# Two adjacency products and a sparse attention correction on one core: staging all columns at once, and product two's chunks placed whole

## What is computed

```python
# layer 0: scores exist only at the pairs; the diagonal is 1e-7, absent edges are -inf
attn = softmax(where(adj == 0, -inf, scores), axis=2)      # 8 heads
x = layernorm(x + (attn.sum(0) / 8) @ x)
# layer 1, on the result
S = (adj + adj.T) * 0.5 + eye;  deg = S.sum(1);  An = deg[:, None]**-0.5 * S * deg[None, :]**-0.5
x = layernorm(x + (adj @ An) @ x)
```

## Time and profile before

| what | us |
|---|---|
| median of 3 runs | 257.16 (256.54 to 257.19) |
| span of the profiled execution | 256.0 |
| PE busy / weight loads | 196.7 / 87.7 |
| DVE busy | 149.1 |
| ACT busy | 73.1 |
| POOL busy | 93.5 |
| bytes read and written in HBM | 25.66 and 8.86 MB, 135 GB/s over the span |

### The profile page before, as it was taken

One profiled execution on the slowest core, in us unless ns is written; L12 is line 12 of the kernel. 1 busy time (PEld: TensorE's weight loads), 2 busy tenths in 40 slices (PEclk: granted clock), 3 DMA queues, 4 the chain that ended last, 5 costly groups with the idle time before them and its releaser, 6 DMA issues.

```text
span 256.0 us, 2880 instructions
## 1 busy us (share of the span) xinstructions
PE 196.7 (77%) x874; PEld 87.7 (34%) x874; DVE 149.1 (58%) x351; ACT 73.1 (29%) x119; POOL 93.5 (37%) x107
## 2 busy tenths in 40 slices
PE   0003999999585376966999999879669999999950
PEld 0001344444132122422564434334224444444420
DVE  7826646429799369945610008769484445387871
ACT  2005384044762698330003130311032222001010
POOL 3677877777778777730011005601010000000000
PEclk9999999999799687995958999999999999999996
DMA  4971886189751399930002001911139100022230
GB/s 148 382 226 25 321 283 172 44 323 289 281 198 52 90 340 300 328 123 28 0 3 82 0 0 30 300 54 41 41 102 305 72 0 3 0 104 102 82 123 24
DMA packets 16623, 34.69 MB, mean 135 GB/s; under 512 B 5148, under 2 KB 5274, under 8 KB 16610
## 3 DMA queue, kind: packets, MB, share of 16 engines
q1 hardware_dynamic: 13074, 30.74, 35.7%
q0 software_dynamic: 3536, 3.79, 5.2%
HBM read 25.66 MB, written 8.86 MB: 135 GB/s over the span
## 4 chain that ended last, share of the span: by engine, by line
POOL 31%; PE 27%; DVE 19%; issue 13%; DMA 5%; ACT 2%; DVEq 1%; POOLq 0%
POOL kept L421 31%; PE ps L598 16%; DVE stats L1129 3%; PE ps L684 3%; DVE xs L1126 3%; DMA kept<-in_adj_t,at_idx 2%; DVE xs L1133 2%; PE ps L664 2%; PE ps L609 2%; PE ps L719 2%; ACT std L587 1%; DMA work<-v_rows 1%; DMA v_rows<-work 1%; DVE mv L1130 1%; PE ps L681 1%
## 5 line engine op out<-in xcount | busy, mean ns | idle before, releaser
L421 POOL DMA_INDIRECT kept<-in_adj_t,at_idx x79 | 79.8, 1010 | 28.5 <-issue 23.8
L598 PE MATMUL ps<-terms,at 128*128 128x512 f16 x264 | 61.4, 392 | 3.2 <-ACT at L494 2.3
L609 PE MATMUL ps<-terms,at 128*128 128x512 f16 x220 | 52.0, 399 | 10.4 <-ACT u L499 10.4
L598 PEld LDWEIGHTS ps<-terms,at 128*128 128x128 f16 x264 | 26.4, 101 | 36.5 <-issue 3.7
L609 PEld LDWEIGHTS ps<-terms,at 128*128 x220 | 22.2, 102 | 39.9 <-issue 16.9
L598 PE MATMUL ps<-terms,bm 128*128 128x512 f16 x110 | 30.4, 446 | 4.3 <-DVE terms L836 4.3
L609 PE MATMUL ps<-terms,bm 128*128 128x512 f16 x132 | 29.3, 379 | 0.0
L598 PEld LDWEIGHTS ps<-terms,bm 128*128 128x128 f16 x110 | 12.1, 112 | 21.7 <-issue 12.9
L609 PEld LDWEIGHTS ps<-terms,bm 128*128 128x128 f16 x132 | 12.8, 98 | 16.4 <-issue 1.7
L553 ACT ACTIVATE u<-ps 128x512 f32<-128x512 f32 x11 | 6.0, 601 | 37.7 <-PE ps L598 25.1
L848 DVE TENSOR_TENSOR bm<-bm,at 128x1408 f16<-128x1408 f16 x11 | 9.8, 890 | 11.6 <-ACT bm L506 11.4
(11 more groups left out here) (222 smaller groups left out, 207.9 us busy)
## 6 DMA issues: line engine op xcount, KB each, us to landing
stage<-in_adj_t SPq DMA_DIRECT2D x10, 677.0 KB, 6.8
stage<-in_adj SPq DMA_DIRECT2D x10, 677.0 KB, 5.0
u_rows<-u SPq DMA_DIRECT2D x10, 257.5 KB
x_rows<-xs SPq DMA_DIRECT2D x10, 256.0 KB
xs<-x_rows SPq DMA_DIRECT2D x10, 256.0 KB
out<-xs SPq DMA_DIRECT2D x10, 256.0 KB
xs<-in_x SPq DMA_DIRECT2D x2, 768.0 KB, 4.7
kept<-in_adj_t,at_idx POOLq DMA_INDIRECT x79
```

Source lines behind the costliest of these rows:

```text
L421: pool.indirect_dma_start(out=kept[:, c:c + 1], out_offset=None, in_=adj_flat, in_offset=bass.IndirectOffsetOnAxis(ap=at_idx[:, c:c + 1], ...
L598: m = pe.matmul(ps[:, i, :], matrix[:, k, i * P:(i + 1) * P], terms[:, s, k, :], start=first and s == 0, stop=last and s == 1)
L609: m = pe.matmul(ps[:, bass.ds(bank_of(i), 1), :].rearrange("p o d -> p (o d)"), matrix[:, k, bass.ts(i, P)], terms[:, s, k, :], start=(k = ...
```

## The change

It has six parts. (1) Each of the 11 column loads has a place of its own (three `stage` slots, four in `u`, five in `bm`), so all are issued right behind x without a wait; the rows use `stage` and `work`. (2) The element-wise load of the diagonal goes; DVE takes it from `at` with a masked product and a reduce per group (`own_entries`). The 11 additions of 2 on the diagonal become three (`add_identity`). (3) DVE makes the gather index before anything else that isn't needed, in 4 instructions in place of 10, and moves the rest of that work, some memsets and `slot_cols` behind the last low term of product one. (4) The scale goes to all partitions by one f32 matmul of ones with a diagonal. (5) Product two's terms are written into `u`, each chunk over its own f32 row, and its results into `xs`; ACT's `high_terms(m)` waits for the stores of that part of `u`. (6) PE does all eleven `bx_step`s and three whole chunks before the ranks, one chunk before the packing, one before q and k, none in loops 2 and 3, and one at the start of loop 4.

```diff
-X_LOADS = [(0, 3), (3, 7), (7, C)]
+X_LOADS = [(0, 4), (4, 8), (8, C)]
-STEPS_TO_RANKS, STEPS_TO_PACK = 6, 9
-BEFORE_QK, AFTER_QK, IN_LOOP2, IN_LOOP3, IN_LOOP4 = 1, 1, 1, 1, 1
-ROWS_V = (1, 3, 5)
+BEFORE_RANKS, BEFORE_PACK, BEFORE_QK, IN_LOOP4 = 3, 1, 1, 1
+ROWS_V = (3, 7)
+STAGE_T = [("u", 0), ("u", 1), ("u", 2), ("u", 3), ("bm", 0), ("bm", 1), ("bm", 2), ("bm", 3), ("bm", 4), ("stage", 0), ("stage", 1)]
+STAGE_R = [("stage", 2), ("work", 0), ("work", 1), ("work", 2), ("stage", 0), ("stage", 1), ("stage", 2), ("work", 0), ("work", 1), ("work", 2), ("stage", 0)]
...
+        def z_term(i, s):
+            return u[:, i, 0:H].bitcast(f16)[:, s * H:(s + 1) * H]
...
 # SP
             for k in range(C):
-                if k >= STAGES:
-                    j = k - STAGES
-                    sp.wait_ge(at_odd if j % 2 else at_even, j // 2 + 1)
                 rows = P if k < C - 1 else TAIL
-                sp.dma_start(stg[0:rows, k % STAGES, 0:N], adj_t[k * P:k * P + rows, :]).then_inc(stage_in[k % STAGES], 16)
-            sp.dma_start(a_ii[:, 0:C - 1]..., bass.AP(tensor=adj_t.tensor, ...)).then_inc(aii_in, 16)
-            sp.dma_start(a_ii[0:TAIL, C - 1:C], ...).then_inc(aii_in, 16)
+                sp.dma_start(staged(STAGE_T[k])[0:rows, :], adj_t[k * P:k * P + rows, :]).then_inc(col_in[k], 16)
+            for r in range(C):
+                before = [q for q in range(r) if STAGE_R[q] == STAGE_R[r]]
+                if before:
+                    rows_cast(sp, before[-1])
+                elif STAGE_R[r] in STAGE_T:
+                    k = STAGE_T.index(STAGE_R[r])
+                    sp.wait_ge(at_odd if k % 2 else at_even, k // 2 + 1)
+                rows = P if r < C - 1 else TAIL
+                sp.dma_start(staged(STAGE_R[r])[0:rows, :], adj[r * P:r * P + rows, :]).then_inc(row_in[r], 16)
...
 # ACT
-            act.wait_ge(scale_ready, 1)
             for k in range(C):
-                act.activation(terms[:, 0, k, :], xs[:, k, :], ACT.Copy, scale=scale[:, 0:1]).then_inc(x_hi, 1)
                 if k % 2 == 0:
                     (cast of column k)
+                if k == 0:
+                    act.wait_ge(scale_ready, 1)
+                else:
+                    act.activation(terms[:, 0, k, :], xs[:, k, :], ACT.Copy, scale=scale[:, 0:1]).then_inc(x_hi, 1)
...
-            for r in (0, 2, 4):
+            for r in ROWS_S[:6]:
                 adj_rows(r)
             for i in GROUP_A:
                 ax_evacuate(i, i)
+            for r in ROWS_S[6:]:
+                adj_rows(r)
...
             def high_terms(m):
+                u_kept(act, m)          # waits for the stores of u of this part
                 act.wait_ge(x1_ready, PARTS[m][1])
                 for i in range(*PARTS[m]):
-                    act.activation(terms[:, 0, i, :], xs[:, i, :], ACT.Copy, scale=dinv_x[:, i:i + 1]).then_inc(xt_hi, 1)
-            adj_rows(6)
-            adj_rows(7)
-            adj_rows(8)
+                    act.activation(z_term(i, 0), xs[:, i, :], ACT.Copy, scale=dinv_x[:, i:i + 1]).then_inc(xt_hi, 1)
             ax_evacuate(6, ax_bank(6))
-            adj_rows(9)
-            adj_rows(10)
-            ax_evacuate(7, ax_bank(7))
             roots_of(0)
             dense_norm(0)
+            ax_evacuate(7, ax_bank(7))
+            high_terms(0)
             ax_evacuate(8, ax_bank(8))
-            ax_evacuate(9, ax_bank(9))
-            ax_evacuate(10, ax_bank(10))
-            high_terms(0)
             roots_of(1)
             dense_norm(1)
             high_terms(1)
+            ax_evacuate(9, ax_bank(9))
+            ax_evacuate(10, ax_bank(10))
             roots_of(2)
...
 # PE
-            for k in range(0, STEPS_TO_RANKS):
-                pe.wait_ge(bm_ready, k + 1)
+            for k in range(C):
+                if k in (0, 6):
+                    pe.wait_ge(bm_ready, 1 if k == 0 else 3)
                 bx_step(k)
+            bx_chunks(0, BEFORE_RANKS)
             pe.wait_ge(base_in, 1)
             (ranks)
-            pe.wait_ge(bm_ready, C)
-            for k in range(STEPS_TO_RANKS, STEPS_TO_PACK):
-                bx_step(k)
+            bx_chunks(BEFORE_RANKS, BEFORE_PACK)
             (packing)
-            for k in range(STEPS_TO_PACK, C):
-                bx_step(k)
             pe.wait_ge(l1_slots, tiles)
-            bx_chunks(0, BEFORE_QK)
+            bx_chunks(BEFORE_RANKS + BEFORE_PACK, BEFORE_QK)
...
 # DVE, behind the memsets of raw, xs, ones, at and col_a
+            dve.wait_ge(pairs_in, 32)
+            main(dve.tensor_scalar(pg[:, :, :], raw[:, :, :], 0.0, float(N), ALU.is_lt, ALU.mult))
+            main(dve.tensor_tensor(pf[:, :, :], raw[:, :, :], pg[:, :, :], ALU.add))
+            main(dve.scalar_tensor_tensor(ok2[:, :], pf[:, :, 1], float(N), pf[:, :, 0], ALU.mult, ALU.add))
+            dve.tensor_scalar(at_idx[:, :], ok2[:, :], 0.0, float(N * N - 1), ALU.max, ALU.min).then_inc(idx_ready, 1)
...
+            (behind the low terms of product one: memsets of bm, row_a, ones16, onecol, rank16;
+             two16 = 2 * ident16; ok, ok2, code; slot_cols)
...
+            def add_identity(lo, hi):
+                dve.wait_ge(v_step, main.n)
+                dve.tensor_tensor(blocks(bm, lo, hi), blocks(bm, lo, hi), each(two16, hi - lo), ALU.add).then_inc(bm_ready, 1)
+            def own_entries(lo, hi):
+                own = ...
+                main(dve.tensor_tensor(own, blocks(at, lo, hi), each(ident16, hi - lo), ALU.mult))
+                main(dve.tensor_reduce(a_ii[:, lo:hi], own, AX.X, ALU.add))
...
-            two_way(0, 6)
+            for lo, hi in ((0, 6), (6, C - 1), (C - 1, C)):
+                own_entries(lo, hi)
+            two_way(0, 7)
+            add_identity(0, 6)
             dense_rows(0)
-            two_way(6, C)
+            two_way(7, C)
+            add_identity(6, C - 1)
+            add_identity(C - 1, C)
             dense_finish(0)
```

More of the change, by code:

```diff
@@ L116, in build, with staged, columns_in, rows_in @@
         row_x0 = words[:, 18 * P + 4 * H:18 * P + 5 * H]
-        stg = stage[:, :].rearrange("p (s n) -> p s n", s=STAGES)
+        homes = {
+            "stage": stage[:, :],
+            "work": work[:, :].bitcast(f32),
+            "u": u[:, :, :].rearrange("p c d -> p (c d)"),
+            "bm": bm[:, :, :].rearrange("p c n -> p (c n)").bitcast(f32),
+        }
+        def staged(place):
+            home, slot = place
+            return homes[home][:, slot * NP:slot * NP + N] if home == "stage" else homes[home][:, slot * N:(slot + 1) * N]
+        def columns_in(eng, k):
+            eng.wait_ge(col_in[k], 16)
+        def rows_in(eng, r):
+            eng.wait_ge(row_in[r], 16)
         w_sb = stage[:, 0:2 * HC * H].rearrange("p (w c n) -> p w c n", w=2, c=HC)
@@ L380, in _ @@
                     rows = P if i < C - 1 else TAIL
-                    sp.dma_start(u_rows[i * P:i * P + rows, :], u[0:rows, i, :]).then_inc(u_stored, 16)
+                    sp.dma_start(u_rows[i * P:i * P + rows, :], u[0:rows, i, :]).then_inc(u_stored[m], 16)
                 for i in range(lo, hi):
@@ L453, in _ @@
             pool.wait_ge(x1_stored, 16 * C)
-            pool.wait_ge(u_stored, 16 * C)
+            for m in range(len(PARTS)):
+                u_kept(pool, m)
             take_indices(0, tiles + 1, row_i)
@@ L552, in bx_evacuate @@
                 act.wait_ge(bx_done, i + 1)
-                act.activation(u[:, i, 0:H], ps[:, i % 5, :], ACT.Copy).then_inc(bx_out, 1)
-            act.wait_ge(u_stored, 16 * C)
-            bx_evacuate(0)
+                act.activation(xs[:, i, :], ps[:, i % 5, :], ACT.Copy).then_inc(bx_out, 1)
+            act.wait_ge(x1_stored, 16 * C)
+            act.wait_ge(xt_lo, C)
+            early = len(AHEAD) + BEFORE_RANKS + BEFORE_PACK
+            for i in range(early):
+                bx_evacuate(i)
             act.activation(warm[:, :], eps_c[:, :], ACT.Exp).then_inc(warmed, 1)
@@ L566, in _ @@
                 act.activation(k_sb, ps[:, 6, :], ACT.Copy).then_inc(l1_k_sb, 1)
-            for i in AHEAD[1:]:
+            for i in range(early, C - IN_LOOP4):
                 bx_evacuate(i)
@@ L579, in _ @@
                 with act.If(t < 1):
-                    for i in BESIDE[-IN_LOOP4:]:
+                    for i in range(C - IN_LOOP4, C):
                         bx_evacuate(i)
@@ L590, in _, with together_step @@
         def _(pe):
-            def together_step(k, first, last, bank_free, ready, matrix, done, chunks=GROUP_A):
+            def together_step(k, first, last, bank_free, ready, matrix, term, done, chunks=GROUP_A):
                 ready(k)
@@ L597, in together_step @@
                     for s in range(2):
-                        m = pe.matmul(ps[:, i, :], matrix[:, k, i * P:(i + 1) * P], terms[:, s, k, :],
+                        m = pe.matmul(ps[:, i, :], matrix[:, k, i * P:(i + 1) * P], term(k, s),
                                       start=first and s == 0, stop=last and s == 1)
```

(3 more changed lines are left out.)

204 lines of the change are left out of this document (97 added, 107 removed).

## The result

| | before | after |
|---|---|---|
| median, us | 257.18 (256.54 to 258.71, 4 runs) | 280.28 (279.51 to 281.22, 4 runs) |
| ratio | | 1.089, 95% interval 1.0847 to 1.0933 |
| span of the profiled execution | 256.0 | 278.7 |
| ranks on PE start | 117.58 | 143.26 |
| from there to the end of the span | 138.4 | 135.4 |

The change costs 23.1 us; 281.0 was forecast. The page's chain that ended last, by engine, answers to the earlier trace rows: POOL is gone from it.

The account below looks back on a forecast made before the run. The gathers bound the ranks by 4.4 us over the dense work; the change makes PE's product two decide. Ranks at 143.4 plus tail 136.8 give span 280.2, plus 1.1: 281 us, range 265 to 289.

Parts of the forecast that it names:

- column block 10 lands: Last column block, 74 rows, behind ten blocks on the same two DMA engines: lands at 48.5 (46 to 51), against 50.9.
- moved work and diagonal done: On DVE after product one's last low term: small instructions and slot_cols 4.8, on-chip diagonal 2.8, ending at 59.0.
- step 4: Product two on PE: waits for low term 4 behind dense_rows(2), evacuations 9 and 10 and part 1's stores, until 113.3.
- The tail: From the ranks on PE to the span's end: 138.4 - 3.9 - 3.3 + 5.6 = 136.8.
- The cold clock: PE restarting at half clock in the tail, in loops 2 to 4 and product three: costs 5.6 in all, 0 to 8.
- Rival 1: Stores land before ACT asks (win 4), columns come 3 earlier, PE stays warm (win 5.6): about 268; chance 0.13.
- Rival 4: Nothing moves: ranks at 119 by a mix of rivals 1 and 2; chance 0.02.
- Rival 2: No gap on PE, faster: product two from 78.4, ranks at 117.5, 255.4 in all; chance 0.09.
- Rival 3: Product two's terms in u read slower: 10% on 242 matmuls adds 5.3, giving 287; chance 0.06.

Follow-up runs that it names:

- evacuate first: The changed kernel with ACT evacuating chunk 8 ahead of high_terms(0) and chunks 9 and 10 ahead of high_terms(1): 266.93 us, ratio 1.0375.
- the run with three chunks back: The changed kernel with the three whole chunks before the ranks moved behind q and k and into loops 2 and 3: 262.83 us, ratio 1.0233.
- the order of before: The changed kernel with part 6 alone undone, PE's order of product two and ACT's evacuations as before the change: 264.05 us, ratio 1.0281.
- all four edits together: The changed kernel with evacuations first, weights behind part 0's stores, all 74-row transfers cut, three chunks behind the ranks and loop 4's chunk late: 245.27 us, ratio 0.9552.
- the index first: The kernel before the change with part 3's gather index alone, four instructions ahead of x: 255.13 us against 256.9.
- the third wait gone: The changed kernel with part 6 undone, plus DVE's edge count and ranks moved ahead of its last low terms: 257.66 us against 256.9.

## Why the prediction was right, step by step

| step | forecast | measured |
|---|---|---|
| product one starts on PE | 22.7 | 22.07 |
| column block 10 lands | 48.5 | 44.9 |
| last low term of product one ends | 51.4 | 47.7 |
| moved work and diagonal done | 59.0 | 56.0 |
| dense_rows(0) done | 77.4 | 73.7 |
| dense_finish(0) done | 84.1 | 79.7 |
| stores of part 0 of `u` landed | 93 | 89.8 |
| product two starts | 101.7 | 98.5 |
| step 4 starts | 113.3 | 112.3 |
| 70 matmuls, then three chunks | 15.4, 14.7 | 16.8, 14.5 |
| ranks | 143.4 | 143.3 |
| ranks to the end of the span | 136.8 | 135.4 |

**What held.** The mechanism is the forecast's: more PE work ahead of the ranks, uncovered because high_terms(0) waits for the stores with the evacuation queued behind it. The experiments take it apart as the text did: 15.9 for the order, 13.0 for what was queued behind the store wait. The two are not parts of one sum (together they are more than 23.1): undoing either leaves less to win from the other. Of the signs that were named, POOL left the chain, PE waited for no rank, 66 matmuls of the chunk line stand ahead of the ranks, and no step of product two came before 90. The gathers begin at 4.7, 3.2 sooner where 2.4 was taken, and the last is issued at 107.9; when it landed the profile doesn't show, as DVE comes to it only at 123.0 and doesn't wait. L694 (now L704) took 3.12, not about 4.

**One term of the sum was off by 3.6**, the landing of column block 10. The tail of x was there 1.25 sooner than the 17.34 that was taken over (DVE's reduce of it starts at 16.09). The ten blocks behind it were priced at the 299 GB/s of the earlier trace rows, and the loads, now without a wait for a slot, moved faster, in the changed kernel's window:

```profile
18.00:32.00 14.00, 10.70 (x38) 4.56 (x39) 11.90 (x22) 9.93 (x15) 10.65 (x12) 1.00 1.02 390
```

The Trainium skill's 435 GB/s (DMA: Bandwidth & Descriptors, Specifications) is not reached in it either; the measurement lies between the two rates that the prediction set against each other. The forecast's range for the block, 46 to 51, missed the 44.9. All that DVE did after it was priced well: from 51.4 to 84.1 is 32.7, and from 47.7 to 79.7 is 32.0.

**The error was made good further on.** Step 4 was expected 1.2 after the end of the first four; it came 3.42 after. The forecast had named what it hangs on, the stores of part 1 and two evacuations behind high_terms(1), and had the time 1.0 too late. And the 70 matmuls behind that gap were priced at the full clock: they took 16.83, where they take 15.33 behind a gap of 1.30 (evacuate first). So 143.3 against 143.4 is in part luck: the forecast was 3.2 too late at the start of product two, and had 2.2 too little for the gap ahead of step 4 and 1.4 too little for the restart.

**The tail** was 1.4 shorter than forecast. Ranks to the end of the packing took 9.8 (forecast 9.9), packing to q and k 8.6 (7.9). The cold clock cost less: in loop 2 1.6 in place of 2.2 (3.12 for 1.98, and 0.5 on the pair ahead of it), product three 1.15 in place of 2.2 (36.0 from the first matmul with dz to the start of the chunk line, 209.50 to 245.53; 34.9 before). That the loop 2 part is the clock is shown by its granted clock of 0.66 and by the run with three chunks back, in which the 3.12 are 1.98 again; for product three no run took it apart.

**What the forecast did not see.** The third wait (DVE's edge count behind low terms 9 and 10) lets the ranks start at 123 at the earliest in the changed kernel. It had no price here, being hidden, and it shows only in the order of before, where it is worth about 6. With earlier terms it goes by itself: with all four edits together the low terms are done by 99.9, 11 us ahead of the gathers.

**The rivals.** Rival 1, the milder drag, had its columns (3.6 sooner, where it asked for 3), but not its other two conditions: ACT still stood 5.07 in front of the stores, and PE did go cold. Rival 4 is out with ranks at 143.3. Rival 2 needed the first low term by 79. With four edits PE could start at 80.45 and did product two in one piece; the change as made had it at 98.3, 19 late, and what kept it away was the 74-row block, the store wait and the order. The chain through DVE, which the prediction held to leave nothing before 90, was as long as it said; what it took as given was where the chain begins, at the landing of that block, 11 us later than it had to. Rival 3 is out: a chunk whose terms lie in `u` takes 4.92 at full clock (143.31), where the earlier trace rows has 4.91.

## What to carry to other kernels

A buffer used in place saves space and makes a wait on whoever still reads it, here a store that is bound to be late. Put that wait last among what its engine has to do: two swapped calls were worth more than half of the loss. Before work is moved ahead of a serial point, compare its length with the idle time there (4.4 us here, against 25.5 of matmuls); the same work in the gaps behind the point was free here and kept the clock up. And look at a profile for stretches in which several engines stand still while the DMA share is half or less: blocks of 74 rows were behind it, and cutting them in two was worth 11.3 us.

## What the runs showed of the hardware that was not expected

- A load of 74 rows moved far slower than one of 128, as the prediction had it from the earlier trace rows; what it didn't ask is whether that can be helped. Cut into 64 and 10 rows, the same bytes landed 10.7 us sooner behind the same ten loads, with the tail of x cut as well.
- A gap does not by its length alone tell what the clock does behind it. Behind gaps of 1.30 and 2.14 us the 70 matmuls took 15.3 us, behind 2.63, 2.69 and 3.42 they took 16.8 to 17.0; but in the earlier trace rows the 2.82 ahead of L733 left the next 22 at 4.91. In loop 3 of the kernel before, 44 matmuls behind a gap of 1.45 and one small pair took 9.67; with the index first and with the third wait gone, behind 1.40 and that pair, they took 11.35 and 11.38. What else decides wasn't tried.
- The time from the last gather's issue to its landing is not fixed: 6.26 before, 5.39 with the index first, 2.37 with everything together, where hardly any other transfer ran beside it (DMA share 0.02 from 104.5 to 112.3).
- In one set of runs PE stood mostly 1.5 to 3 us at "issue" between single matmuls while the gathers ran, at a granted clock of 0.50, in all four kernels that were traced there; of the kernel before there is only the time, 314.9. With the index first, in a window from 60 to 100, PE was busy 8.77 us of 40:

```profile
60.00:100.00 40.00, 8.77 (x15) 1.55 (x15) 7.28 (x18) 1.42 (x2) 30.36 (x32) 0.50 0.23 74
```

The kernels are the same as in the runs in which this didn't happen, and for two of them the chip has the same number in the record. So neither the program nor, by that number, the chip explains it; what held PE there stays open.
